# A vision layer with routed experts: tokens listed per expert image by image, weighing runs right behind the scores, stacks loaded head by head

## The reference

```python
h = einsum(patches, Wp) + bp + position                     # 8 images x 1024 tokens x 256
x = layernorm(h)
q, k, v = split((layernorm(x) * gamma + beta) @ W_qkv.T)     # 8 heads of 32
gate = sigmoid(x @ W_gate.T + b_gate)
attn = softmax(q k^T / sqrt(32))                             # 1024 x 1024 a head
h = h + x + ((attn^T v) * gate) @ W_final.T + b_final
x = layernorm(h)
H = gelu(x @ W1 + b1)                                        # hidden rows of 1024
probs = softmax(H @ Wg + bg);  assign = argmax(probs)        # 8 experts
h = h + probs[assign] * (H @ Wd[assign] + bd[assign])       # each token by its own expert
```

## Time and profile before

| | |
|---|---|
| median of 3 runs | 1827.46 us |
| profiled execution, its own time | 1824.39 us |
| span | 1822.6 us |
| PE busy | 1631.2 us, 90% |
| DVE busy | 1201.0 us, 66% |
| ACT busy | 943.0 us, 52% |
| POOL busy | 307.8 us, 17% |

### The profile page before, as it was taken

The page is one execution under the profiler, slowest core; times in us unless marked ns, Lnnn a source line. Parts: engine busy times, 40 slices in busy tenths (PEclk is TensorE's granted clock), DMA queues, the critical chain, the costliest instruction groups (busy, mean ns, idle before and its releaser), DMA issues.

```text
span 1822.6 us, 29454 instructions
## 1 busy us (share of the span) xinstructions
PE 1631.2 (90%) x11124; PEld 1125.0 (62%) x11124; DVE 1201.0 (66%) x1904; ACT 943.0 (52%) x1560; POOL 307.8 (17%) x231
## 2 busy tenths in 40 slices
PE   8796999999999999999999999998885707999998
PEld 6463556556646665665657456645443506999998
DVE  2376686868777776777677767776666496444443
ACT  0465655756575657567565756575663331222222
POOL 0202000200200020002001000200000081555554
PEclk9798999999999999999999999999999858999999
DMA  4313235242604251342325141603330462666663
GB/s 162 87 53 69 43 94 132 57 99 64 144 19 111 68 147 23 106 117 81 87 67 131 42 110 53 162 5 89 80 83 20 118 163 90 199 202 204 208 198 129
DMA packets 121218, 187.57 MB, mean 103 GB/s; under 512 B 11883, under 2 KB 86265, under 8 KB 120956
## 3 DMA queue, kind: packets, MB, share of 16 engines
q1 hardware_dynamic: 104652, 120.42, 26.7%
q0 software_dynamic: 16000, 63.98, 10.9%
q10 hardware_dynamic: 432, 1.31, 0.2%
HBM read 84.98 MB, written 51.38 MB: 75 GB/s over the span
## 4 chain that ended last, share of the span: by engine, by line
PE 68%; DVE 18%; issue 7%; ACT 5%; DMA 1%; SPq 1%; POOL 0%; POOLq 0%; DVEq 0%; ACTq 0%
PE ps L509 12%; PE ps L752 11%; PE ps L523 11%; PE ps L476 8%; DVE nmax L1066 6%; ACT pr L854 3%; PE ps L740 3%; PE ps L559 3%; PE ps L536 3%; PE ps L497 3%; PE ps L580 2%; PE ps L582 2%; PE ps L581 2%; PE ps L543 1%; PE ps L450 1%
## 5 line engine op out<-in xcount | busy, mean ns | idle before, releaser
L1066 DVE TENSOR_REDUCE nmax<-ps 128x1 f32<-128x1024 f32 x512 | 623.7, 1221 | 216.7 <-PE ps L509 209.8
L854 ACT ACTIVATE pr<-ps,nmax 128x1024 f32<-128x1024 f32 x512 | 570.7, 1115 | 287.1 <-DVE nmax L1066 282.2
L509 PE MATMUL ps<-st 96*128 96x512 f32 x1024 | 399.6, 474 | 70.5 <-ACT pr L854 60.8
L509 PEld LDWEIGHTS ps<-st 96*128 96x128 f32 x1024 | 168.2, 191 | 266.5 <-ACT pr L854 128.6
L523 PE MATMUL ps<-pr,vs 128*32 128x256 f32 x4096 | 271.7, 386 | 11.5 <-DVE vs L957 11.5
L752 PE MATMUL ps<-wd,hg 128*128 x1728 | 224.9, 287 | 0.0
L752 PEld LDWEIGHTS ps<-wd,hg 128*128 128x128 f32 x1728 | 212.2, 192 | 0.0
L523 PEld LDWEIGHTS ps<-pr,vs 128*32 128x32 f32 x4096 | 108.8, 109 | 153.4 <-issue 70.4
L890 ACT ACTIVATE hg<-ps 128x512 fp32r<-128x512 f32 x144 | 78.6, 596 | 239.6 <-PE ps L740 234.8
L476 PE MATMUL ps<-wp,xt 128*128 128x256 f32 x672 | 172.8, 378 | 0.0
L823 ACT ACTIVATE ht<-ps,bf 128x512 f32<-128x512 f32 x128 | 88.3, 690 | 129.8 <-PE ps L582 129.8
(11 more groups left out here) (129 smaller groups left out, 1885.6 us busy)
## 6 DMA issues: line engine op xcount, KB each, us to landing
st<-qk SPq DMA_DIRECT2D x192, 256.0 KB, 5.1
xt<-x_in SPq DMA_DIRECT2D x58, 384.0 KB, 3.1
token_rows<-staged_b SPq DMA_DIRECT2D x64, 256.0 KB, 4.1
token_rows<-staged_a SPq DMA_DIRECT2D x64, 256.0 KB, 4.1
token_rows<-hres POOLq DMA_DIRECT2D x8, 1024.0 KB, 5.2
wd_raw<-w_down SPq DMA_DIRECT2D x64, 128.0 KB, 3.0
pr<-x_in SPq DMA_DIRECT2D x6, 384.0 KB, 9.0
rows<-token_rows,slot_from POOLq DMA_INDIRECT x72
```

What stands on the lines that cost most here:

```text
L509: last = mm(ps[:, 2 * (k % SR) + j, :], stq[:, hh, i * P:(i + 1) * P], stk[:, hh, j * 512:(j + 1) * 512], start=True, stop=True)
L854: actv(pr[:, k % PR, :], ps[:, 2 * (k % SR):2 * (k % SR) + 2, :].rearrange("p a n -> p (a n)"), ACT.Exp, bias=nmax[:, k % 16:k % 16 + 1], ...
L1066: V.reduce_max(nmax[:, k % 16:k % 16 + 1], ps[:, 2 * (k % SR):2 * (k % SR) + 2, :].rearrange("p a n -> p (a n)"), AX_X, negate=True).then_ ...
```

## The change

1. **Routing image by image.** The logits of an image are kept in `rl` with the bias added. VectorE does the choice, the probability and the place of the image's 1024 tokens in 14 small pieces `route(r, i)` in the second half of the next image's attention (`ROUTE_AT`); the exponential stands on ScalarE at k = G_STEPS + 11, and one product of 72 columns with two passes (`prefix`) on TensorE at k = G_STEPS + 15. Each expert has a fixed region of 64 rows of 128 in a DRAM table, and GpSimd writes the token numbers there by 8 indirect DMAs of 128 single numbers for each image (`place`). The probability goes into the token's row in DRAM (`store_prob`), which grows from 1280 to 1284 numbers. For the last image all this comes after its router. Then one indirect DMA gathers the used table rows, TensorE turns them, and VectorE makes the 71 slots' indices. The running sums and all `select` and `sort` rounds are gone.
2. **Expert weights loaded earlier.** The 16 pieces are loaded, split high and split low during the last image: `high_down(0..3)` in its attention, `4..8` before its router, `9..15` between the gelus of its router.
3. **Slots.** 71 are worked through, not 72.
4. **Weighing.** The pieces of `weigh` stand right behind the score of their step, ahead of the step's other products, and one step later.
5. **Stacks.** `load_stack` waits head by head for the last score that read the head's stack, not once for all.

```diff
-ROW = HID + D
+ROW = HID + D + 4
+PROB = HID + D
+USED = SLOTS - 1
...
+        PREFIX_AT = G_STEPS + 15
+        DOWN_AT = {G_STEPS + 12 + 4 * m: m for m in range(4)}
...
         WEIGH_AT = {k: [(i, j) for i in range(15) if i != 7 for j in range(4)
-                        if k == min(4 * i + 5 + j // 2 * 2, (i // TILES + 1) * G_STEPS - 1)] for k in range(STEPS)}
+                        if k == min(4 * i + 6 + j // 2 * 2, (i // TILES + 1) * G_STEPS - 2 + j // 2)] for k in range(STEPS)}
...
             def load_stack(b, g):
                 hold(sp, "qk_lo", b * 8 + 4 * (g + 1))
-                hold(sp, "score_mm", b * STEPS + g * G_STEPS)
                 for hh in range(4):
+                    wait(sp, "score_mm", b * STEPS + g * G_STEPS - 3 + hh)
...
+            def store_prob(b):
+                wait(sp, "prob_ready", b + 1)
+                sp.dma_start(rows_view[b, :, :, PROB:ROW], prob[:]).then_inc(S["prob_out"], 16)
+
+            def load_down(m):
+                i = m % WD_BUFFERS
+                wait(sp, "wd_low", m + 1 - WD_BUFFERS)
+                piece = w_down[m].rearrange("(i n) k d -> k n i d", n=BLK)
+                for k in range(P // BLK):
+                    sp.dma_start(wd_raw[k * BLK:(k + 1) * BLK, i], piece[k]).then_inc(wd_in[i], 16)
...
                 if before:
                     for u in range(4):
                         store_hidden(b - 1, u)
+                    store_prob(b - 1)
             over_images(sp, image)
-            for u in range(4):
-                store_hidden(IMAGES - 1, u)
...
+            sp.wait_ge(S["emb_mm"], IMAGES * TILES)
+            sp.dma_start(bd_raw, b_down).then_inc(S["bd_raw_in"], 16)
+            sp.wait_ge(S["h_sum"], IMAGES)
+            sp.wait_ge(S["g_mm"], 4 * IMAGES)
+            for m in range(8):
+                load_down(m)
+            load_down(8)
+            load_down(9)
+            store_hidden(IMAGES - 1, 0)
+            load_down(10)
+            load_down(11)
+            store_hidden(IMAGES - 1, 1)
+            load_down(12)
+            load_down(13)
+            store_hidden(IMAGES - 1, 2)
+            load_down(14)
+            load_down(15)
+            store_hidden(IMAGES - 1, 3)
+            store_prob(IMAGES - 1)
             sp.wait_ge(S["bd_low"], 1)
             sp.wait_ge(S["bd_zero"], 1)
...
+            def place(b):
+                wait(pool, "table_in", 16)
+                wait(pool, "addr_ready", b + 1)
+                for t in range(TILES):
+                    nc.gpsimd.indirect_dma_start(
+                        table_flat, bass.IndirectOffsetOnAxis(addr_i[:, t:t + 1], 0),
+                        tid[:, b * TILES + t:b * TILES + t + 1], None,
+                        bounds_check=EXPERTS * ALL_TILES * P - 1, oob_is_err=False).then_inc(S["table_out"], 16)
...
                 if after:
                     front(b + 1, 1 - par)
+                if before:
+                    place(b - 1)
             over_images(pool, image)
+            for m in range(4):
+                split_down(m)
             root_3(IMAGES - 1)
             store_rear(IMAGES - 1, (IMAGES - 1) % 2)
             pool.wait_ge(S["bd_high"], 1)
+            nc.gpsimd.tensor_tensor(bd_parts[:, 1], bd_raw, bd_parts[:, 0].bitcast(F32), ALU.subtract
+                                    ).then_inc(S["bd_low"], 1)
+            for m in range(4, WD_PIECES):
+                split_down(m)
+            pool.wait_ge(S["ff_mm"], 16 * IMAGES)
             nc.gpsimd.memset(bd[:].bitcast(F32), 0.0).then_inc(S["bd_zero"], 1)
+            place(IMAGES - 1)
...
+            pool.wait_ge(S["table_out"], 16 * ALL_TILES)
+            nc.gpsimd.indirect_dma_start(tab, None, table, bass.IndirectOffsetOnAxis(row_i[0:SLOTS, 0:1], 0)
+                                         ).then_inc(S["tab_in"], 16)
...
+            def prefix(r):
+                wait(pe, "r_oh", r + 1)
+                mm(spare(0)[:, 0:(TILES + 1) * EXPERTS], up[:], oh[:, GUARD:].rearrange("p t e -> p (t e)"),
+                   start=True, stop=False)
+                mm(spare(0)[:, 0:(TILES + 1) * EXPERTS], ones[:].bitcast(F32),
+                   run[:, 2, GUARD:].rearrange("p t e -> p (t e)"), start=False, stop=True).then_inc(S["r_mm"], 1)
...
                     score(b, k)
+                    for gi, j in WEIGH_AT[k]:
+                        weigh(b, gi, j)
...
+                    if before and k == PREFIX_AT:
+                        prefix(b - 1)
                     if after and k in QK0_AT:
                         j, c = QK0_AT[k]
                         if j == 0 and c == 0:
                             wait(pe, "tr_read", b * 8 + 16)
+                            wait(pe, "r_read", b)
...
                         values(b + 1, 0, VALUE_AT[k])
-                    for gi, j in WEIGH_AT[k]:
-                        weigh(b, gi, j)
...
+            def high_down(m):
+                if m == 0:
+                    wait(act, "ha_ready", IMAGES)
...
+                i = m % WD_BUFFERS
+                wait(act, wd_in[i], (m // WD_BUFFERS + 1) * 16 * (P // BLK))
+                actv(wd_piece(0, m), wd_raw[:, i], ACT.Identity).then_inc(S["wd_high"], 1)
...
+                        if b == IMAGES - 1 and k % 2 == 1 and HC * hf + k < 14:
+                            high_down(9 + (HC * hf + k) // 2)
...
+                    if before and k == PREFIX_AT - 4:
+                        exponentials(b - 1)
+                    if not after and k in DOWN_AT:
+                        high_down(DOWN_AT[k])
...
             over_images(act, image)
+            act.wait_ge(S["bd_raw_in"], 16)
+            actv(bd_parts[:, 0], bd_raw, ACT.Identity).then_inc(S["bd_high"], 1)
+            for m in range(4, 9):
+                high_down(m)
             router(IMAGES - 1)
+            exponentials(IMAGES - 1)
...
+            ROUTE_AT = {G_STEPS + 4: (0, 1), G_STEPS + 5: (2,), G_STEPS + 6: (3,), G_STEPS + 7: (4,), G_STEPS + 8: (5,),
+                        G_STEPS + 9: (6,), G_STEPS + 10: (7,), G_STEPS + 13: (8,), G_STEPS + 14: (9,),
+                        PREFIX_AT + 1: (10,), PREFIX_AT + 2: (11,), PREFIX_AT + 3: (12,), PREFIX_AT + 4: (13,)}
...
+            for i in range(8):
+                route(last, i)
+            for i in (10, 11, 12, 13):
+                route(last, i)
+            for i in (8, 9):
+                route(last, i)
...
```

More of the change, by code:

```diff
@@ L422, in _ @@
                 gather_rows(s)
-            for s in range(SLOTS):
+            for s in range(USED):
                 scatter_rows(s)
-                if 1 <= s <= SLOTS - RING:
+                if 1 <= s <= USED - RING:
                     gather_rows(s + RING - 1)
@@ L757, in _ @@
             pe.wait_ge(S["wd_low"], WD_PIECES)
-            for s in range(SLOTS):
-                if s + 1 < SLOTS:
+            for s in range(USED):
+                if s + 1 < USED:
                     turn_rows(s + 1)
@@ L838, in image @@
                     wait(act, "fin_mm", b * 4)
+                if not before:
+                    wait(act, "table_in", 16)
                 for hf in range(2):
@@ L1074, in image @@
                         scale_v(b, SCALE_AT[k])
+                    if before and k in ROUTE_AT:
+                        for i in ROUTE_AT[k]:
+                            route(b - 1, i)
                     if before and k in NORM_AT:
@@ L1169, in _ @@
-            over_pairs(dve, ALL_TILES // 16, select)
-            for e in range(EXPERTS):
-                link(V.scalar_tensor_tensor(slot_f[:, (e + 1) % 2, :], sst[:], cnt[:, 1, e:e + 1], slot_f[:, e % 2, :],
+            last = IMAGES - 1
+            for i in range(8):
[4 more added lines that the diff above has]
+                route(last, i)
+            final_base = base[:, IMAGES % 2, :]
+            wait(dve, "r_read", IMAGES)
```

383 lines of the change are left out of this document (203 added, 180 removed).

## The result

The changed kernel takes 1847.76 us (median of 4 runs, 1847.22 to 1851.11) against 1827.2 us of the kernel before beside it: 1.0128 times as long, 95% interval 1.0095 to 1.016. Forecast were 1814 us and a range of 1788 to 1833: it is slower, and beyond the range. The profiled execution took 1851.11 us, span 1849.2 us, 26.6 us more than the 1822.6 of before. In a later group of runs, on chip 2 (the chip of the first is not on record), the same kernel took 1879.73 us where the kernel before took 1826.31 (1.0297, 1.0279 to 1.0316); that belongs to the result as well.

A forecast was written before the change was run, and what follows sets the result against it. The prediction took the chain as mostly TensorE, with the score round pacing the last image and VectorE busy in the placing. Terms -58.6 - 3.9 + 44 + 5 = -13.5 from 1827.5 gave 1814 us, range 1788 to 1833.

The forecast's parts named there:

- part 3: Expert weights loaded under the last image: ScalarE's waits for pieces not yet loaded cost +44 us (+30 to +59).
- part 4: Attention loops: placing pieces, exponential and projection's wait cost 1.0 us an image, weighing first gains 2; +5 us in all.
- a): Last image's attention, step 44: ScalarE waits for the first weight piece, loaded behind a store; +9 us (7 to 11).
- b): Last image, steps 59 to 63: value scaling on VectorE meets four GpSimd low parts; +2 us (0 to 5).
- c): Before the last router: ScalarE waits for weight piece 8, +4.7 us (3 to 7); slower clock afterwards, +1.5.
- d) to f): Last router, behind gelus 3, 7 and 3 of the second half: ScalarE waits for weight pieces; +10, +7, +10 us.
- d): Last router, behind gelu 3: ScalarE waits for weight piece 10, loaded behind a hidden-block store; +10 us (7.5 to 12).
- Part 1: Placing, from last logits to first expert product: 89.4 us shrinks to 30.8, -58.6 us (-63 to -46).
- Part 2: Experts' stage: 71 slots instead of 72, bound by TensorE, so one whole slot goes; -3.9 us.
- Rival 4: Placing scatters go one at a time, 39 us for 10, giving 1843 us; chance 0.08.
- Rivals 1 to 3: Short part 3 waits, 1790 us (0.15); weighing first pays everywhere, 1794 (0.12); VectorE bounds second halves, 1840 (0.10).

The follow-up runs named there:

- after_spaced: The changed kernel with the scatters of images 0 to 6 spread over steps 52 to 62: 1838.24 us, ratio 1.0074 to the kernel before.
- pool_order: The changed kernel with GpSimd's low parts of the expert weights moved behind the last value scaling and normalising: 1864.47 us.
- before_weigh: The kernel before with only the weighing moved right behind a step's scores and one step later: 1825.81 us, ratio 1.001.
- spaced_pairs: Changed kernel, loads and weight store reordered, low parts moved, scatters spread; last image's scatters in pairs, each awaiting the previous pair's landing: 1794.44 us.
- after_again: The changed kernel, unaltered, run again in a later group on chip 2: 1879.73 us, ratio 1.0297 to the kernel before.
- place_moved: The changed kernel with each image's eight scatters issued one image later, in the first half instead of the second: 1873.55 us.

## Why the prediction was wrong

By stages, us. "After" is the changed kernel's profiled execution, which the forecast was for; in after_spaced the scatters of images 0 to 6 don't stand in a pile. The forecast's column adds up its terms (it took part 3's 44.2 as 44). The first expert product is the first in the trace; the chain counts it from 0.3 us later, before and after.

| stretch | before | after | difference | after_spaced | forecast |
|---|---|---|---|---|---|
| to the last maximum (part 4, a, b) | 1389.8 | 1421.0 | +31.2 | +18.7 | +16 |
| to the last copy of the turned norm (c) | 25.4 | 41.6 | +16.2 | +21.2 | +4.7 |
| to the last logits (c's slower clock, d to f) | 34.6 | 70.0 | +35.4 | +35.1 | +28.5 |
| to the first expert product (part 1) | 89.0 | 36.5 | -52.5 | -53.1 | -58.6 |
| to the end (part 2) | 283.8 | 280.1 | -3.6 | -3.2 | -3.9 |
| sum | | | +26.6 | +18.7 | -13.3 |

In after_spaced the scaling that waits for the low parts (5.14 us) is the last one, behind the last maximum. So b) is in the first line of "after" and in the second of after_spaced.

- **Part 1** was right in its chain (addresses 4.5, measured 4.6; scatters 10.4, measured 10.0; gathers to product 9.9, measured 9.8). One term was mis-sized: landing, table and turn, taken as 6 us within 4 to 16, cost 11.6; and 0.9 us from the addresses to the first scatter I had left out. The 2.0 us for a landing in that term stood in no row, and the runs show 5.2 us at least behind a scatter. The lower end of -63 doesn't come out of the terms either, which give -61.
- **Part 2** was right: slots of 3.86 us, 71 of them.
- **Part 3** failed most, though each wait stood where it was put. a) forecast 9: from the maximum of step 46 to that of step 48 it takes 13.6 us instead of 3.3, +10.4. b) forecast 2, at most 5: the value scaling took 5.75 us instead of 0.29, +5.5. d) to f) 27 and c)'s 1.5 against 35.4: ScalarE waited 11.26, 11.38 and 11.10 us, because a piece came 7 us behind its first issue, not 4.2. In d) its four loads took 3.2 us to be issued (1.3 before) and the last landed 3.7 us later (2.8 before). That 4.2 came from a time in which nothing else moved; here the loads follow 1 MB of hidden blocks on their queue, which I had priced at 0.5. That this store makes up the difference is likely, not shown.
- **Step c) is the step that failed in kind.** I laid ScalarE's wait for piece 8 there, 4.7 us. VectorE's normalising ended later than that wait: 15.56 us for 2.93. The stage grew by 16.2 us. I had weighed GpSimd's subtractions against VectorE in b) only, as one operation waiting for one, and not asked which other VectorE work falls under them. The Trainium skill, "SBUF — State Buffer", section "Who interferes with whom", says that `tensor_scalar`, the operation of the normalising, can take both port pairs as well and then contends with GpSimd, and that the loser is blocked for a whole instruction. The trace shows the two exclude each other (the normalising is short again in pool_order), and here the block goes beyond one instruction: 5.6 us over subtractions of 2.3 us each, and 13 us over five of them. In the kernel before it was one subtraction each time, which is what I had read; the row that I named for it in b) has only one SBUF input, so it doesn't show the rule for two, and L1123 above does.
- **Part 4** came out at +7.7 up to the last image's step 32 in after_spaced, where the forecast had +6 for six images. The pieces cost 1.4 us an image (second halves of images 1 to 6, after_spaced against before_weigh), forecast 1.0. The 0 for weighing first was luck: it does move things, by 0.8 us in each middle and 0.7 in each gap, and gets them back in the second halves. **The 0 for `place` was wrong**, the second step that failed in kind. GpSimd was idle there, as I wrote, but eight scatters in a row can stop ScalarE, VectorE and TensorE: in the profile of the forecast's run one gap of 25.0 us instead of 19.6 is plain, by the ratios it may be 10 us, and on chip 2 it was 41.
- **Rival 4** had the right object and the wrong mechanism: the scatters do go together, and it is their going together that hurts. Rivals 1 to 3 are out: the waits were long, weighing first alone gives nothing, and the pieces cost 1.4 us an image, not 4.5.

## What to carry to other kernels

A copy or a load moved under other work is free only if its whole queue is: list what stands ahead of it on each in-order queue (the store that waits for a turn, the low part that waits for a copy), and send loads ahead of stores that wait. Where GpSimd runs several subtractions in a row, VectorE's products of two SBUF tiles and its normalising can wait for the end of the run, while its maxima, which read PSUM, don't (1.22 us each beside the first two subtractions, as elsewhere): put such runs under work of that kind. Spread indirect DMAs with small pieces. And expect more than a price read in a quiet stretch where the stretch is busy.

With these points, and the weighing of steps 31 and 63 put back, the same change is worth 2.9% (1771.66 us) instead of costing 1.3%.

## What the runs showed of the hardware

- A scatter of 128 pieces of 4 bytes takes 1.0 us of GpSimd and 1.3 us from one to the next. GpSimd waits 5.2 to 7.1 us from the end of a pair until both count as landed (spaced_pairs), and 7.7 to 10.1 us behind eight in a row (all other kernels), so it is a price for the pile, not for each.
- Eight such scatters without a pause stop ScalarE, VectorE and TensorE for some 3 us in six of seven images in after_again, and VectorE once for 10.9 us (place_moved); spread or as plain transfers they don't. Weight loads issued from 2.4 us behind them take 9.8 us to land (median) instead of 5.1.
- A VectorE instruction with two SBUF inputs, or a normalising, can wait through GpSimd instructions that follow each other without a pause: 5.75 us for a 0.29 us operation, 15.56 us for 2.93. In the kernel before they waited for one at a time (2.71 us for 0.69).
